# A two-layer graph network on one core: three staged chunks instead of twelve, late rows copied before their scatter, one row tile moved between two scatters, an output stage three quads deep

## The reference

```
h = relu(layernorm(x))                        # x: 100000 nodes x 128
x = x + attention(h, src, dst)                # layer 0, 4 heads of 32
#   x_l = h @ W_l + b_l ; x_r = h @ W_r + b_r
#   edges: 50000 (src -> dst, sorted by dst) and a self loop of each node
#   e = leaky_relu(x_l[s] + x_r[d]) . att ; softmax over the edges of d ; sum of alpha * x_l[s] ; + bias
h = relu(layernorm(x))
x = x + convolution(h, edge_attr, edge_weight, src, dst)      # layer 1
#   msg = (h @ W_in)[dst] * (ssp(edge_attr @ Wf1 + bf1) @ Wf2 + bf2) * edge_weight
#   agg = segment_sum(msg, src) ; ssp(agg @ Wo1 + bo1) @ Wo2 + bo2 ; ssp(z) = softplus(z) - log 2
```

## Time and profile before

| | before |
|---|---|
| median of 3 runs | 3322.52 us (3319.03 to 3331.44) |
| profiled execution | 3332.83 us, its span 3331.0 us |
| busy: PE / DVE / ACT / POOL | 76% / 74% / 66% / 58% of the span |
| stages, from the first of a stage to the next | dense about 0 to 645 us, edge to 1792, message to 2953, output to 3331 |

### The profile page before, as it was taken

The page is one execution under the profiler, slowest core; times in us unless marked ns, Lnnn a source line. Parts: engine busy times, 40 slices in busy tenths (PEclk is TensorE's granted clock), DMA queues, the critical chain, the costliest instruction groups (busy, mean ns, idle before and its releaser), DMA issues. The chain is left out here.

```text
span 3331.0 us, 58371 instructions
## 1 busy us (share of the span) xinstructions
PE 2544.2 (76%) x16674; PEld 1760.3 (53%) x16674; DVE 2454.0 (74%) x6275; ACT 2194.7 (66%) x4803; POOL 1916.5 (58%) x1633
## 2 busy tenths in 40 slices
PE   6776777788887877787886777777777777758887
PEld 5554555444443444444444665666555565547776
DVE  7554555678887877887787778777878778737776
ACT  6655666667777777777775555555555555549998
POOL 2564555267766666766752777777777777720000
PEclk9877899989999999999998889788899899979999
DMA  7665566333333333333333666666666666679998
GB/s 239 241 229 187 212 215 214 118 117 130 127 126 116 130 116 129 118 128 116 124 102 102 117 116 116 115 113 117 119 117 119 116 117 118 114 261 404 424 422 350
DMA packets 323596, 558.99 MB, mean 168 GB/s; under 512 B 135552, under 2 KB 211828, under 8 KB 285794
## 3 DMA queue, kind: packets, MB, share of 16 engines
q1 hardware_dynamic: 226290, 448.50, 40.1%
q0 software_dynamic: 97200, 109.30, 16.6%
HBM read 324.12 MB, written 242.20 MB: 170 GB/s over the span
## 5 line engine op out<-in xcount | busy, mean ns | idle before, releaser
L665 POOL DMA_INDIRECT sum_dram<-b_sum,b_at x392 | 641.1, 1636 | 233.3 <-issue 117.2
L589 POOL DMA_INDIRECT a_xd<-in_x,index x344 | 361.5, 1051 | 162.4 <-issue 100.0
L580 POOL DMA_INDIRECT a_xs<-in_x,index x344 | 364.5, 1060 | 146.8 <-issue 101.6
L598 POOL DMA_INDIRECT x_dram<-a_xo,index x196 | 211.4, 1079 | 290.7 <-DVE a_xo L900 191.7
L1330 PE MATMUL bank<-wl,turned 128*128 128x128 f32 x1568 | 263.8, 319 | 74.4 <-ACT turned L1106 54.4
L802 DVE TENSOR_TENSOR d_x<-bank,d_x 128x512 f32<-128x512 f32 x196 | 134.7, 687 | 239.0 <-remote 142.6
L1330 PEld LDWEIGHTS bank<-wl,turned 128*128 128x128 f32 x1568 | 222.5, 219 | 134.4 <-ACT turned L1106 89.5
L1109 ACT ACTIVATE d_n<-d_x,stat_d_shift,stat_d_rstd 128x128 f32<-128x128 f32 x686 | 283.3, 485 | 0.2 <-DVE stat_d_shift L701 0.2
L1453 PE MATMUL bank<-b_rows,b_same 128*128 128x128 bf16 x4704 | 279.9, 219 | 0.6 <-ACT b_sum L1246 0.6
L1486 PE MATMUL bank<-wo,f_ssp_out 128*128 128x128 f32 x1568 | 225.3, 287 | 55.9 <-DVE f_ssp_out L1055 51.9
L1453 PEld LDWEIGHTS bank<-b_rows,b_same 128*128 128x128 bf16 x4704 | 265.1, 98 | 0.6 <-issue 0.6
(11 more groups left out here) (191 smaller groups left out, 7025.7 us busy)
## 6 DMA issues: line engine op xcount, KB each, us to landing
d_x<-in_x SPq DMA_DIRECT2D x49, 1024.0 KB
x_dram<-d_x SPq DMA_DIRECT2D x49, 1024.0 KB
out<-d_x SPq DMA_DIRECT2D x49, 1024.0 KB, 7.6
sum_dram<-zero SPq DMA_DIRECT2D x48, 1024.0 KB
d_x<-x_dram SPq DMA_DIRECT2D x45, 1024.0 KB, 12.0
d_n<-sum_dram SPq DMA_DIRECT2D x25, 1024.0 KB, 9.1
x_end_dram<-a_xo SPq DMA_DIRECT2D x98, 256.0 KB
b_x<-x_end_dram SPq DMA_DIRECT2D x98, 256.0 KB
```

The costliest lines, as they stand in the source:

```text
L580: pool.indirect_dma_start(a_xs[t % DEPTH][:, j * F:(j + 1) * F], None, x, column(t, j)).then_inc(gathered[t % GSEM], 16)
L589: pool.indirect_dma_start(a_xd[t % DEPTH][:, j * F:(j + 1) * F], None, x, column(t, TILES + j)).then_inc(gathered[t % GSEM], 16)
L598: pool.indirect_dma_start(x1_dram, column(t, 2 * TILES + j), a_xo[t % 4][:, j * F:(j + 1) * F], None, bounds_check=bound, oob_is_err=False ...
L665: pool.indirect_dma_start(sum_dram, bass.IndirectOffsetOnAxis(ap=b_at[s][:, j:j + 1], axis=0), b_sum[s][:, j * F:(j + 1) * F], None, compu ...
```

## The change

`STAGED` goes from 12 to 3: nine chunks, 72 gathers, leave the list that runs beside the dense stage and join the gathers between the early scatters of the edge stage; 18 stores to `stage_dram` and 18 loads from it are gone. `EARLY` goes from (2, 2) to (2, 1): every second chunk scatters one row tile in the edge stage and three in the message stage. In the message stage ACT copies the late rows of `b_x` into a new tile `b_xo`, two buffers as well, and POOL scatters from there. So the load of `b_x` waits for that copy, not for the landing of a scatter; the wait for the landing moves to ACT's next copy into the same buffer and, on SP, behind the loads of `b_x` and `b_end`, ahead of `sidx`. In the output stage the second multiply stands three quads behind the turn, with four `f_ssp_out` tiles. The loads into `f_pre` wait for the last `b_sum` too. `a_xd`'s first twelve instead of eight buffers lie ahead of `f_pre` in memory.

```diff
--- before.py
+++ after.py
@@ -44,10 +44,10 @@
 SLOPE = 0.2
 SKIP = 1 << 20
 PRE = 8
-EARLY = (2, 2)
+EARLY = (2, 1)
 DEPTH = 24
 GSEM = 4
-STAGED = 12
+STAGED = 3
 
 ALU = mybir.AluOpType
 ACT = mybir.ActivationFunctionType
@@ -207,6 +207,7 @@
             b_w = at2("b_w", [P, C])
             b_src = at2("b_src", [P, C])
             b_y = at2("b_y", [P, TILES * F])
+            b_xo = at2("b_xo", [P, TILES * F])
             b_n = at("b_n", [P, TILES * F])
             b_h = at("b_h", [P, C])
             b_f = at("b_f", [P, P])
@@ -230,11 +231,11 @@
             f_abs_out = at2("f_abs_out", [P, 512])
             f_exp_out = at2("f_exp_out", [P, 512])
             f_ln_out = at2("f_ln_out", [P, 512])
-            f_ssp_out = at2("f_ssp_out", [P, 512])
+            f_ssp_out = [at(f"f_ssp_out{i}", [P, 512]) for i in range(QUADS)]
             f_sums = d_n + [at(f"f_sums{i}", [P, J * F]) for i in range(RX - RN)]
 
         a_xs = [sb(f"a_xs{i}", [P, TILES * F]) for i in range(DEPTH)]
-        a_xd = [sb(f"a_xd{i}", [P, TILES * F]) for i in range(DEPTH - 4 * (PRE - RX))]
+        a_xd = [sb(f"a_xd{i}", [P, TILES * F]) for i in range(DEPTH // 2)]
         with ExitStack() as place:
             f_pre = [place.enter_context(nc.sbuf_tensor(f"f_pre{i}", [P, J * F], F32)) for i in range(PRE - RX)] + d_x
         a_xd += [sb(f"a_xd{i}", [P, TILES * F]) for i in range(len(a_xd), DEPTH)]
@@ -278,7 +279,7 @@
         x1_scattered = sems("x1_scattered"); added = sems("added")
         ones_set = sem("ones_set"); b_six = sem("b_six"); b_sumdif = sem("b_sumdif"); b_sq = sem("b_sq")
         b_var = sem("b_var"); b_logv = sem("b_logv"); b_rstd = sem("b_rstd"); b_shift = sem("b_shift")
-        b_norm = sem("b_norm"); b_y_ready = sem("b_y_ready")
+        b_norm = sem("b_norm"); b_y_ready = sem("b_y_ready"); b_xo_ready = sem("b_xo_ready")
         b_fa_turned = sem("b_fa_turned"); b_f_ready = sem("b_f_ready"); b_z1 = sem("b_z1")
         b_abs_done = sem("b_abs_done"); b_exp_done = sem("b_exp_done"); b_ln_done = sem("b_ln_done")
         b_s1_ready = sem("b_s1_ready"); b_turned = sem("b_turned"); b_h_ready = sem("b_h_ready")
@@ -426,10 +427,13 @@
                     sp.sem_inc(sync_step, 1)
                     sp.wait_ge(b_masked, t - 1)
                     sp.sem_inc(sync_step, 1)
-                    sp.wait_ge(x1_scattered[s], late(s) * turn(k, u - 2))
+                    sp.wait_ge(b_xo_ready, t - 1)
                     sp.sem_inc(sync_step, 1)
                 sp.dma_start(b_x[s][:, :], x1_end_dram[bass.ds(NC - 1 - t, 1), :, :].rearrange("o p f -> (o p) f")).then_inc(b_x_ld[s], 16)
                 sp.dma_start(b_end[s][:, :], ends[:, bass.ds(TILES * (NC - 1 - t), TILES)]).then_inc(b_x_ld[s], 16)
+                if t0 >= 2:
+                    sp.wait_ge(x1_scattered[s], late(s) * turn(k, u - 2))
+                    sp.sem_inc(sync_step, 1)
                 sp.dma_start(sidx[s][:, :], index[:, bass.ds(12 * (NC - 1 - t) + 8, 4)]).then_inc(sidx_ld[s], 16)
                 if t0 >= 2:
                     sp.wait_ge(b_fa_turned, t - 1)
@@ -483,6 +487,7 @@
                 sp.wait_ge(f_out, QUADS * g + QUADS)
                 sp.dma_start(node_rows(out, g), d_x1[slot % RN][:, :]).then_inc(out_stored[slot % RN], 16)
 
+            sp.wait_ge(b_sum_ready, NC)
             for g in range(PRE):
                 sp.dma_start(f_pre[g][:, :], node_rows(x1_dram, g)).then_inc(f_x1_ld[g // BATCH], 16)
             for s in range(2):
@@ -647,11 +652,11 @@
             def scatters(k, u):
                 s = u % 2
                 pool.wait_ge(sidx_ld[s], 16 * turn(k, u))
-                pool.wait_ge(b_x_ld[s], 32 * turn(k, u))
+                pool.wait_ge(b_xo_ready, 2 * k + u + 1)
                 pool.sem_inc(pool_step, 1)
                 for j in range(EARLY[1 - s], TILES):
                     pool.indirect_dma_start(x1_dram, bass.IndirectOffsetOnAxis(ap=sidx[s][:, j:j + 1], axis=0),
-                                            b_x[s][:, j * F:(j + 1) * F], None,
+                                            b_xo[s][:, j * F:(j + 1) * F], None,
                                             bounds_check=bound, oob_is_err=False).then_inc(x1_scattered[s], 16)
 
             def adds(k, u, first=False):
@@ -1049,10 +1054,10 @@
             def f_ssp(c, q, c0):
 
                 dve.wait_ge(f_ln, c + 1)
-                if c0 >= 2:
-                    dve.wait_ge(f_y, c - 1)
-
-                dve.scalar_tensor_tensor(out=f_ssp_out[q % 2][:, :], in0=bank[q][:, :], scalar=cols[:, 6:7],
+                if c0 >= QUADS:
+                    dve.wait_ge(f_y, c - 3)
+
+                dve.scalar_tensor_tensor(out=f_ssp_out[q][:, :], in0=bank[q][:, :], scalar=cols[:, 6:7],
                                          in1=f_ln_out[q % 2][:, :], op0=ALU.max, op1=ALU.add).then_inc(f_s, 1)
 
             def f_rows(c, q, slot, m, c0):
@@ -1072,10 +1077,10 @@
             def f_group(g, slot, m, g0):
                 for q in range(QUADS):
                     f_ssp(QUADS * g + q, q, QUADS * g0 + q)
-                    if q >= 2:
-                        f_rows(QUADS * g + q - 2, q - 2, slot, m, QUADS * g0 + q - 2)
+                    if q >= 3:
+                        f_rows(QUADS * g + q - 3, q - 3, slot, m, QUADS * g0 + q - 3)
                     elif g0:
-                        f_rows(QUADS * g + q - 2, QUADS + q - 2, (slot - 1) % RX, m if slot else m - 1, QUADS * g0 + q - 2)
+                        f_rows(QUADS * g + q - 3, QUADS + q - 3, (slot - 1) % RX, m if slot else m - 1, QUADS * g0 + q - 3)
 
             for g in range(PRE + RX):
                 f_group(g, g % RX, g // RX, g)
@@ -1084,7 +1089,7 @@
                     f_group(m * RX + i, i, m, RX)
             for g in range((1 + ROUNDS) * RX, NG):
                 f_group(g, g % RX, g // RX, g)
-            for n in (2, 1):
+            for n in (3, 2, 1):
                 f_rows(QUADS * NG - n, QUADS - n, (NG - 1) % RX, (NG - 1) // RX, QUADS * NG - n)
 
         @block.scalar
@@ -1205,6 +1210,10 @@
                 s = u % 2
                 t = 2 * k + u
                 st = stat_e[s]
+                act.wait_ge(b_x_ld[s], 32 * turn(k, u))
+                if t0 >= 2:
+                    act.wait_ge(x1_scattered[s], late(s) * turn(k, u - 2))
+                act.activation(b_xo[s][:, early(1 - s):], b_x[s][:, early(1 - s):], ACT.Copy).then_inc(b_xo_ready, 1)
                 act.wait_ge(b_shift, t + 1)
                 if t0 >= 1:
                     act.wait_ge(b_turned, t)
@@ -1483,7 +1492,7 @@
                     pe.wait_ge(f_out, c - 3)
                 pe.wait_ge(f_s, c + 1)
                 for j in range(TILES):
-                    last = pe.matmul(bank[4 + q][:, j * F:(j + 1) * F], f_ssp_out[q % 2][:, j * P:(j + 1) * P], wo2[:, :],
+                    last = pe.matmul(bank[4 + q][:, j * F:(j + 1) * F], f_ssp_out[q][:, j * P:(j + 1) * P], wo2[:, :],
                                      start=True, stop=True)
                 last.then_inc(f_y, 1)
 
@@ -1491,8 +1500,8 @@
                 for q in range(QUADS):
                     c, c0 = QUADS * g + q, QUADS * g0 + q
                     f_turn(c, q, slot, m, c0)
-                    if c0 >= 2:
-                        f_second(c - 2, (q - 2) % QUADS, c0 - 2)
+                    if c0 >= 3:
+                        f_second(c - 3, (q - 3) % QUADS, c0 - 3)
 
             for g in range(RX):
                 f_group(g, g, 0, g)
```

## The result

The changed kernel takes 3275.17 us (median of 4 runs, 3264.98 to 3290.18) where the kernel before took 3323.79: a ratio of 0.9864, 95% interval 0.984 to 0.9888. That is 48.6 us less; the sum had said 17 less.

What follows compares the result with a forecast made beforehand. No engine bounds the whole; each stage has its own limit: gathers (dense), chunk loop (edge), mostly GpSimd (message), transfers (output). Terms −84 + 21 + 44 + 2 = −17 from the median 3322.5 give 3305 us; forecast's own range 3280 to 3325, overall 3240 to 3370.

Steps and rivals of the forecast that it cites:

- Dense stage, −84: Dense stage: 72 gathers fewer shorten the 42 groups from 521.6 to 438 us, 84 us gained, bounds 44 to 114.
- Edge stage, +21: Edge stage: 72 more gathers cost 26 us, fewer loads save 5, so 21 us longer.
- 0.37 us each: Edge stage: mean price of a gather over the 496 already there; for 72 more, 26 us.
- which its 138 us of waits take: Edge stage: GpSimd's net 33 us more work, after 49 fewer early scatters, fits into its 138 us of waits.
- Message stage, +44: Message stage: 49 more late scatters +34, the copy +16, the end −6: 44 us longer, bounds −26 to +111.
- so +16: Message stage: 98 copies on ACT at 0.5 us, 49 us, count only where the chunk loop bounds, about a third.
- In the sum I count nothing for it: Message stage: loading b_x before scatters landed shortens DVE's and SP's waits, but SP's wait only moves; gain counted 0.
- −6: End of message stage: the 11.96 us stall of the last adds goes, the first load comes 2 to 3 us later.
- Output stage, +2: Output stage: transfers bound it, so the third quad gains 0; one quad more at the end costs 2 us.
- The first, that the message stage pays: Message stage: early load of b_x breaks the loop, −26 instead of +44, time 3235 us; chance 0.20.
- Rival 2: Message stage: third scatter and copy stand in series and count in full, +111, time 3372 us; chance 0.17.
- rival 4: Dense stage: a gather costs only its bytes, gain just 22 to 44 us, time 3345 to 3367; chance 0.05.

Runs made afterwards that it cites:

- f1: The changed kernel as it is, run again on the chip of 3321 us: ratio 0.9881 to the kernel before.
- f4: The changed kernel with STAGED = 12 instead of 3: ratio 0.9945 to the kernel before.
- f3: The changed kernel with EARLY = (2, 2) instead of (2, 1): ratio 0.9992 to the kernel before.
- e2: The kernel before with EARLY = (2, 1) alone, without the copy: ratio 0.9902 to the kernel before.
- e1: The kernel before with STAGED = 3 alone: ratio 1.0002 to the kernel before.
- e4: The kernel before with the output stage three quads deep alone: ratio 0.9977 to the kernel before.
- f2: The changed kernel without the copy, scatters out of b_x and SP's wait ahead of its load as before: ratio 0.9923 to the kernel before.
- e3: The kernel before with the copy b_xo alone, two row tiles in every chunk, EARLY = (2, 2): ratio 0.9971 to the kernel before.

## Why the prediction was wrong in size

**Dense stage, −84: right and a little small.** Measured −96 in the profile, −95 by the means of five and five over all chips. Groups with six gathers took 11.0 us, by the sum 10.8; the price of 9.5 for four gathers, halfway between one and six, was too high: the sixteen groups with three or four took 8.55. That is 15 us more gain, of which the larger groups gave back some. The Trainium skill, "DMA: Bandwidth & Descriptors", section "Queues, rings and completion order", says that each DMA engine takes turns between its queues packet by packet; the estimate of 22 us that I had worked out from it, by bytes, did not come. Nor do bytes set the price elsewhere: even scatters that write no row cost 1.16 us each.

**Edge stage, +21: right by luck, from two errors.** Measured +15 in the pair of profiles, +14 by the means. But the step "0.37 us each" is wrong: 72 gathers cost 79 us on one chip and 103 on another, not 26. The mean over the gathers already there divides the stretch by too many, if the first ones hide and further ones don't, as they do in the dense stage. And the step "which its 138 us of waits take" is wrong: 45 early scatters left out gave 50 and 56 us there, where I had nothing. GpSimd's waits for `a_xo` were 138.0 us before and 166.3 after, when it had more to do: they absorbed nothing.

**Message stage, +44: the step that failed.** Measured +15.5 for the 94 chunks and +13 with their head and tail. Of the sum's three terms the first, 34 us for 49 more scatters, holds: 34 on the chip of 3321 us with the copy (runs f1 and f4 against f3), 46 on the slow one without it (e2 against e1 and e4). The second, "so +16" for the copy, has the wrong sign: −8 on either chip (f1 against f2, e3), and −8 and −12 us by the medians of the timed runs. The copy itself takes 0.40 to 0.52 us on ACT, as I had it. What failed is the overlap beside it, "In the sum I count nothing for it": I had seen that `b_x` would be loaded earlier and counted it at nothing because SP's wait only moves behind two loads. It was those two loads that VectorE waited for, 179.9 us in the 94 chunks before and 60.9 after. The reason was not all wrong: `b_goes` and `b_w` do stand behind the moved wait, and VectorE's new 86 us for them go far to explain why so little of the 119 us came through. From +16 to −8 is 24 us, most of the 32 by which the medians missed the sum. The third term, "−6" for the wait ahead of the last adds, was about −3 (from the end of the 94 chunks to the first `f_ssp_out` 59.8 us before and 56.5 after), and its reason did not come: the adds still wait 11.46 us while the 8 MB for `f_pre` are loaded. The later start of these loads was not run by itself.

**Output stage, +2.** +2.1 in the profile, −3.5 alone, 0.9977 with an interval that takes in 1. ACT's waits for PE are 27.6 us after, where they were 27.1: the third quad did not fill them, so the expectation that the transfers bound the stage stands. The lower bound of −9 had a slip: 7.40 − 7.23 is 0.17 us a group and not 0.21, so −7.

**The rivals.** The first, that the message stage pays, had the mechanism of the copy right, and GpSimd's floor as its bound was not reached (11.58 us a chunk, floor 11.2). Rival 2 did not come: no wait ahead of ACT's copy shows in the trace, though SP's moved wait did hold up the loads behind it. Nor did rival 3, the edge stage's +77, or rival 4, a gather that costs its bytes. The signs of being wrong that the prediction names, a dense gain below 44 us or a chunk under 11.4 or over 12.1, did not come either: they left room for an error of this size. The two profiled executions lie 68 us apart, 51 more than the sum: 31 of them are the message stage's with its tail, 12 the dense stage's, 6 the edge stage's, 2 lie ahead of them. The medians lie 49 apart; the other 19 are how two executions scatter, and no stage can be named for them.

## What to carry to other kernels

Take the count of indirect DMAs on a path, not their bytes, and price a further one by its marginal cost in that stage, as one run with some more of them shows; the mean over those already there gave 0.37 us where it was 1.1 to 1.4. A moved operation has two prices, one where it goes and one where it leaves: here 45 scatters left out of the edge stage were worth more than the whole move of 72 gathers, which alone gave nothing. And a copy that frees a buffer early can pay although it stands in the loop, if the load behind it is what the loop waits for. Look then at what still stands behind the wait that was moved: here it took back most of the gain.

## What the runs showed of the hardware

A GpSimd scatter that moves no row costs its stage 1.16 to 1.2 us beside TensorE's work, as one of 64 KB does, and about the same GpSimd time in memsets costs a tenth. TensorE's results reach VectorE late: 227 us of waits in the dense stage with 84 scatters more, 117 in the changed kernel, 109 with memsets. Before and after the change most of the long waits end 1.2 to 1.7 us behind the end of a run of indirect DMAs. The added scatters were measured on the chip of 3321 us and the memsets on that of 3330; the waits are in the profiles of all chips where the kernel before takes 3321 to 3368 us. On two chips where it takes 3000 the waits are gone (6.5 us) and the dense stage's granted clock is 1.00 instead of 0.83 to 0.92. What makes the chips differ, and by what way an indirect DMA delays TensorE's signal, was not found. On the faster ones the changed kernel itself was not run. Its gain in the dense stage rests on waits that don't exist there, and in the edge stage GpSimd is the bound there and gets more to do by the change, so its ratio of 0.986 belongs to the slower ones.
